# Pacing the expert weight loads: one pair of transfers in flight in a mixture-of-experts kernel

## The reference, cut to what matters

```python
x = x + jnp.tanh(g_xattn[0]) * _L0_xattn_ref(_layernorm(x, axis=-1), ctx_2048, ...)
...
topv, topi = jax.lax.top_k(softmax(ht @ router_w), 2)
g = jnp.einsum('td,edf->tef', ht, w_gate)            # E, D, F = 8, 512, 256
u = jnp.einsum('td,edf->tef', ht, w_up)
eo = jnp.einsum('tef,efd->ted', jax.nn.silu(g) * u, w_down)
moe = jnp.einsum('te,ted->td', w_dense, eo)
sh = jax.nn.silu(ht @ sw_gate) * (ht @ sw_up) @ sw_down
return (moe + sh).reshape(b, s, d)
```

## Time and profile before

| | before |
|---|---|
| median of 3 runs | 1470.62 us (1468.78 to 1474.96) |
| the profiled execution's own time | 1475.32 us |
| its span, first to last instruction | 1473.5 us |
| mean granted TensorE clock | 0.992 |
| TensorE matmul busy | 1399.9 us, 95% |
| VectorE / ScalarE / GpSimd busy | 996.1 / 866.4 / 866.0 us |
| DMA moved | 247.93 MB, 168 GB/s |

### The profile page before, as it was taken

How to read it: one execution, slowest core, us unless ns; L and a number is a source line. 1 busy time by engine, 2 the same in 40 slices (tenths; PEclk the granted TensorE clock), 3 DMA queues, 4 the chain that set the end, 5 groups by cost and what they waited for, 6 DMA issues and landing times.

```text
span 1473.5 us, 25166 instructions
## 1 busy us (share of the span) xinstructions
PE 1399.9 (95%) x7290; PEld 720.4 (49%) x7290; DVE 996.1 (68%) x2172; ACT 866.4 (59%) x1720; POOL 866.0 (59%) x1276
## 2 busy tenths in 40 slices
PE   5899999999999999999999999989999899999997
PEld 1223333333333333333333333367788787778886
DVE  5878888888888887887888888746654232333332
ACT  2476777777677776776777776734334333333332
POOL 6446667666877776776777764534213445455553
PEclk9999999999999999999999999999999999999999
DMA  5857677777767767776777665265653876776665
GB/s 141 200 145 203 179 195 199 180 190 181 192 176 192 197 176 176 181 197 169 191 187 189 174 170 141 96 201 129 153 189 80 242 198 137 178 192 109 108 114 79
DMA packets 183329, 247.93 MB, mean 168 GB/s; under 512 B 31045, under 2 KB 105420, under 8 KB 183198
## 3 DMA queue, kind: packets, MB, share of 16 engines
q1 hardware_dynamic: 160846, 208.42, 53.4%
q0 software_dynamic: 18256, 37.38, 13.5%
q10 hardware_dynamic: 4096, 0.53, 0.3%
HBM read 141.85 MB, written 103.88 MB: 167 GB/s over the span
## 4 chain that ended last, share of the span: by engine, by line
PE 61%; issue 13%; DMA 10%; DVE 6%; POOL 4%; ACT 3%; SPq 1%; POOLq 1%; ACTq 1%; DVEq 0%
PE bank L1379 15%; PE bank L1336 14%; PE bank L1307 11%; PE bank L1285 11%; PE bank L1270 4%; DMA pv_d<-arena 3%; DMA out<-xs,ids 2%; POOL xs L745 2%; DVE row_max L857 2%; PE bank L1312 2%; PE bank L1323 2%; DMA arena<-m_rows 2%; ACT arena L1127 2%; PE bank L1274 1%; DMA arena<-pv_d 1%
## 5 line engine op out<-in xcount | busy, mean ns | idle before, releaser
L857 DVE TENSOR_REDUCE row_max<-bank 128x1 f32<-128x512 f32 x1024 | 674.3, 684 | 111.3 <-PE bank L1285 92.9
L1127 ACT ACTIVATE arena<-bank 128x512 f32<-128x512 f32 x1024 | 563.5, 611 | 244.5 <-PE bank L1307 217.0
L1285 PE MATMUL bank<-arena 96*128 96x512 bf16 x1024 | 395.9, 389 | 21.4 <-DVE row_max L857 14.4
L1307 PE MATMUL bank<-arena 98*128 98x512 bf16 x1024 | 390.0, 383 | 11.0 <-ACT arena L1127 4.6
L1336 PE MATMUL bank<-arena 128*32 128x512 f32 x2048 | 276.2, 612 | 1.4 <-ACT arena L1127 1.0
L757 POOL DMA_INDIRECT out<-xs,ids x71 | 112.7, 1588 | 182.8 <-ACT xs L1211 137.6
L1285 PEld LDWEIGHTS bank<-arena 96*128 96x128 bf16 x1024 | 100.8, 98 | 189.5 <-DVE row_max L857 105.0
L1307 PEld LDWEIGHTS bank<-arena 98*128 98x128 bf16 x1024 | 102.9, 101 | 180.4 <-ACT arena L1127 80.0
L1379 PE MATMUL bank<-w_ring,h_hi 128*128 x568 | 184.2, 405 | 0.0
L1200 ACT ACTIVATE arena<-bank 128x256 f32<-128x256 f32 x103 | 39.6, 384 | 192.1 <-PE bank L1379 186.2
L646 POOL TENSOR_TENSOR arena<-arena 128x512 bf16<-128x512 f32 x62 | 71.5, 1154 | 125.0 <-ACT arena L1119 122.4
(11 more groups left out here) (174 smaller groups left out, 1993.6 us busy)
## 6 DMA issues: line engine op xcount, KB each, us to landing
arena<-parts_q SPq DMA_DIRECT2D x64, 256.0 KB
pv_d<-arena SPq DMA_DIRECT2D x32, 512.0 KB, 7.0
w_ring<-split_d SPq DMA_DIRECT2D x60, 256.0 KB
parts_k<-arena SPq DMA_DIRECT2D x96, 128.0 KB
arena<-parts_k SPq DMA_DIRECT2D x32, 384.0 KB
parts_q<-arena SPq DMA_DIRECT2D x96, 128.0 KB
arena<-in_w SPq DMA_DIRECT2D x36, 256.0 KB, 5.7
arena<-in_ctx SPq DMA_DIRECT2D x32, 256.0 KB, 3.1
```

Source lines behind the costliest of these rows:

```text
L857: nc.vector.reduce_max(row_max[b % 2][:, u:u + 1], m_ps[(STEPS * b + u) % M_BANKS][:], AX_X).then_inc(s_mx, 1)
L1127: nc.scalar.activation(probs[group % 3][:, j, :], e_ps[n % E_BANKS][:], ACT.Exp, scale=float(DH) ** -0.5).then_inc(s_exp, 1)
L1285: nc.tensor.matmul(m_ps[n % M_BANKS][:], q_stack[b % 3][0:STACK, h, qt * P:(qt + 1) * P], k_stack[b % 3][0:STACK, h, :], start=True, stop= ...
L1307: nc.tensor.matmul(e_ps[n % E_BANKS][:], k_stack[b % 3][0:SHIFTED, h, kt * P:(kt + 1) * P], q_stack[b % 3][0:SHIFTED, h, :], start=True, s ...
```

## The change

Before each row but the first of an expert, SP waits until the transfers of the rows before it have landed. Two transfers, the high and the low part of a row, are then on their way at a time in place of up to twelve. The order of the transfers, their sizes and the waits ahead of an expert's first row stay.

```diff
                     last = sp.value_load(slot_end[0:1, e - SLOTS:e - SLOTS + 1], min_val=B, max_val=JOBS)
                     sp.wait_ge(s_dn, last)
+                landed = W_ROWS * IN_PLACE + LOADED * (e - IN_PLACE)
                 for r in range(W_ROWS):
+                    if r:
+                        sp.wait_ge(s_wrt, landed + 2 * DMA * r)
                     for part in range(2):
                         sp.dma_start(w_ring[:, e % SLOTS, part, r, :].bitcast(F32), split_d[e - IN_PLACE, part, :, r, :]
                                      ).then_inc(s_wrt, DMA)
```

## The result

| | before | after |
|---|---|---|
| median (12 runs each) | 1469.92 us (1466.65 to 1475.48) | 1463.84 us (1456.03 to 1473.49) |
| ratio | | 0.9945, 95% interval 0.9926 to 0.9965 |
| span of the profiled execution | 1473.5 us | 1462.1 us |

Faster by 0.35 to 0.74%. The prediction was 1461.3 us, range 1457 to 1468.5, with faster the likeliest. The changed file has three more lines, so that L745 of before is L748 here, L757 is L760, L1312 is L1315.

What follows compares the result with a forecast made beforehand. TensorE was taken to set the pace, disturbed only by the loads. The execution's 1475.3 us less 11.7 plus 2.4 gave 1466.0, a gain of 9.3; off the median 1470.6 that made 1461.3 us, range 1457 to 1468.5.

Steps and rivals of the forecast that it cites:

- What bounds it: Routed jobs: TensorE sets the pace, only the ring loads disturb it; 11.7 us lost is the most recoverable.
- The waits cost nothing: SP's 25 added waits: a pair takes about 5 us, a load some 30; cover of 92 and 112 us hides it.
- What pacing gives: GpSimd's gathers and additions beside loads: 0 to 4.8 us of loss stay at four changes of expert, middle 2.4.
- the 1.54 us: Most foreign work one pair in flight can put ahead of a GpSimd transfer; a burst has up to 9.2 us.
- The clock's fall: First load stretch: granted clock at 0.50 for three microseconds after a 2.24 us stall, should go with that stall.
- Taking the gain off the median: Whole time: the gain of 9.3 us subtracted from the median 1470.6, since the profiled execution was 4.7 us above it.
- the forecast itself: Whole time: a gain of 7 to 11.7 us, giving 1459 to 1463.6 us; chance 0.52.
- the first rival: Changes of expert beside loads: 4.8 us stay, gain 6.9, time 1463.7 us; chance 0.22.
- Every boundary pays in full: Each loaded change of expert meets two pairs, each delaying by 1.54 us; 4.8 us stay, time 1463.7; chance 0.22.
- The loads cost less outside of this execution: Routed jobs: the median run lost only 7.0 us to loads, gain 4.6, time 1466.0 us; chance 0.15.
- A pair blocks as long as a burst: Gathers beside loads: each of 30 pairs makes a tile 1.05 us late, 20 us slower, about 1490; chance 0.06.

Runs made afterwards that it cites:

- a pair a job: Changed kernel, each pair also waiting for one more job's down product, so at most one pair a tile; ratio to before 0.9872, again 0.9955 (medians 1480.6, 1474.0 us).

## Why the prediction was right, point by point

**What bounds it: right, and shown.** I had up to 11.7 us to be had from calmer loads. The kernel without loads lost 0.3 us in the routed part, the one before 12.0 and 11.2, the changed one 1.0, 2.9 and 3.3.

**The waits cost nothing: right.** A pair took 4.9 us on average where I had 5 (4.5 to 5.5 in the five loads), expert 3's load 34 where I had 30, and TensorE never waited for a piece. Even single pieces, 4.0 us each, were in time.

**What pacing gives: the mechanism right, a term too large.** I left 2.4 us (0 to 4.8) with the loads and 0.9 of the 11.7 stayed in the first profile; on the other two chips 1.5 to 2.0 without the eighth tile. That is within the 0 to 4.8 but under its middle, as additions came less late than the 1.54 us allowed: at the changes they stepped by 6.00, 5.77, 5.95 and 5.63 us where it is 5.35 with no load, in the predicted 5.4 to 8.4. TensorE's waits for gathers from 1140 to 1320 us were 0.6 us, under the 2.5 named. The clock's fall between 1147 and 1186 went with the stall.

**Taking the gain off the median: this is where the number is off.** The routed part gained 11.0 us between the two profiles, more than the 9.3 forecast, yet the medians differ by 6.1 us; the ratio 0.9945 makes 8.1 us of 1469.9. The median of 1463.84 lies in the range, but 0.2 us outside of the band that I had for the forecast itself (1459 to 1463.6), and nearer to the first rival's 1463.7 than to my 1461.3. The wide range, made for the spread of executions, is what holds it. In the later sets the medians of pairs are 9.5 and 5.4 us under before. The profiles show where such numbers can scatter: up to 14 us between executions in the part ahead of the routed tiles, on one chip. The changed kernel's twelve runs span 17 us, and their time goes roughly with the granted clock: the three fastest (1456 to 1458 us) had a mean of 0.989 or 0.990, two of the three slowest (1467.8 and 1473.5) 0.984. What makes the clock fall more often in some executions wasn't examined.

**The rivals.** *Every boundary pays in full* (4.8 us stay) is out, though its time was all but met: 1 to 2 stay. The shares of the queues, 46.8 and 40.0% with a pair in flight and 15.9 and 85.8% with twelve, don't tell how the engines take turns between them, since pairs leave SP's queue empty for part of the time; what puts the rival out is the routed part's loss. *The loads cost less outside of this execution* is out for the routed part, by the second profile of before. *A pair blocks as long as a burst* is out: no tile away from a change took over 4.79 us in the first profile, and only the eighth and the one behind it in the other two. But the picture behind my sum, that delay grows with what stands ahead, would have priced four pieces at 3 to 7 us, and they cost 13.3. For pairs the terms hold. What the sum lacked for deeper groups, as that one profile reads, is that a paced load lasts into the tiles that must make up for the late addition, and that a stall can cost a fall of the clock on top.

## What to carry to other kernels

When a bulk prefetch with much cover shares the DMA engines with small transfers that have 2 to 3 us of slack, bound what it has in flight, and read from the trace how long it may take: here a load that took nearly twice as long (34.3 us in place of 18.7) cost nothing and gave back 8 to 11 us of stalls. Look also at when it starts: a slot that comes free at a boundary starts the load exactly where the boundary's own wait is. A depth between deep and shallow need not be a safe middle, as four pieces at the change show: sweep it, and judge it by the spacing of the work in the part touched where the whole time varies by more than the effect.

## What the runs showed of the hardware that I had not expected

- Four 256 KB transfers in flight at the change of expert lost as much as twelve (13.3 and 11.2 to 12.0 us), two lost 1 to 3.3, and four begun three tiles later lost 0.7.
- A single 256 KB transfer, waited for each time, took 4.0 us and a pair 4.9 on average with the gathers beside them, so the second piece of a pair costs 0.9 us.
- Four stalls of TensorE, of 2.24 us before, 2.13 and 2.21 with four pieces and 2.04 with a pair a job, were each followed by a tile of 6.41 to 6.45 us in place of 4.79, with a granted clock of 0.50 to 0.61 in the stages behind them.
- The same kernel's median was 1470, 1481, 1491 and 1494 us in four sets on different chips, while its undisturbed routed tile took 4.79 us in all of them.
